# A six-layer decoder on one Trainium2 core: half of the Newton iteration's head pairs no longer cross the TensorE array

## The reference

```
def iterative_inv(mat, n_iter=6):
    I, K = eye(m), mat
    V = swapaxes(K, -1, -2) / denom
    for _ in range(n_iter):
        KV = matmul(K, V)
        V = matmul(0.25 * V, 13 * I - matmul(KV, 15 * I - matmul(KV, 7 * I - KV)))
    return V
SV = matmul(matmul(kernel1, iterative_inv(kernel2)), matmul(kernel3, V))
```

## Time and profile before

| what | value |
|---|---|
| median of three runs | 2584.53 us |
| profiled execution, its own time | 2582.42 us |
| its span | 2580.6 us |
| TensorE busy | 2279.9 us, 88% |
| VectorE busy | 1957.8 us, 76% |
| ScalarE busy | 1443.2 us, 56% |
| GpSimd busy | 360.0 us, 14% |
| mean granted TensorE clock | 0.951 of full |
| ScalarE copies of crossed groups (lines 993, 1004) | 150.9 + 129.5 us |

### The profile page before, as it was taken

One profiled execution on the slowest core, in us unless ns is written; L12 is line 12 of the kernel. 1 busy time (PEld: TensorE's weight loads), 2 busy tenths in 40 slices (PEclk: granted clock), 3 DMA queues, 4 the chain that ended last, 5 costly groups with the idle time before them and its releaser, 6 DMA issues.

```text
span 2580.6 us, 95561 instructions
## 1 busy us (share of the span) xinstructions
PE 2279.9 (88%) x40576; PEld 1845.7 (72%) x40576; DVE 1957.8 (76%) x6185; ACT 1443.2 (56%) x5093; POOL 360.0 (14%) x516
## 2 busy tenths in 40 slices
PE   6589999999999999999999999999999999999875
PEld 4467777777777777777777777777777777777763
DVE  3358887887888887788888777888877788887753
ACT  0346565655665556566555655655565565656531
POOL 0001111111111111111111111111111111111111
PEclk9589999999999999999999999999999999999995
DMA  6000000000000000000000000000000000000000
GB/s 267 5 4 7 9 9 8 9 9 5 7 9 9 9 9 9 5 7 8 8 9 8 9 5 8 8 8 9 8 9 5 8 8 9 9 8 7 4 5 3
DMA packets 29529, 35.73 MB, mean 14 GB/s; under 512 B 3240, under 2 KB 27824, under 8 KB 28464
## 3 DMA queue, kind: packets, MB, share of 16 engines
q1 hardware_dynamic: 29104, 29.62, 3.3%
HBM read 27.51 MB, written 2.10 MB: 11 GB/s over the span
## 4 chain that ended last, share of the span: by engine, by line
PE 44%; DVE 29%; ACT 18%; issue 6%; POOL 1%; DVEq 0%; ACTq 0%; POOLq 0%
PE ps L525 23%; PE ps L528 7%; ACT probs L1079 5%; PE ps L785 3%; ACT ss L993 3%; PE ps L869 3%; PE ps L802 3%; DVE probsT L1322 2%; ACT probs L1027 2%; PE ps L917 2%; ACT ey L1004 2%; DVE small L1227 2%; DVE x_rows L1186 2%; DVE small L1315 2%; DVE qk_v L1310 1%
## 5 line engine op out<-in xcount | busy, mean ns | idle before, releaser
L1027 ACT ACTIVATE probs<-ps,small 128x128 f32<-128x128 f32 x1024 | 282.5, 391 | 70.1 <-DVE small L1315 69.2
L1322 DVE COPY probsT<-ps 128x512 f32<-128x512 f32 x384 | 262.8, 684 | 75.8 <-PE ps L528 72.7
L1112 POOL TENSOR_TENSOR small<-small,weights 128x1 f32<-128x1 f32 x256 | 140.6, 549 | 1178.7 <-DVE small L1175 1178.7
L528 PE MATMUL ps<-weights,probs 128*128 128x128 f32 x1536 | 248.0, 284 | 47.1 <-POOL probs L1123 23.8
L1315 DVE TENSOR_REDUCE small<-ps 128x4 f32<-128x512 f32 x384 | 254.1, 683 | 13.0 <-PE ps L869 8.7
L528 PEld LDWEIGHTS ps<-weights,probs 128*128 128x128 f32 x1536 | 171.3, 142 | 110.4 <-POOL probs L1123 45.0
L1123 POOL TENSOR_TENSOR probs<-probs,small 128x256 f32<-128x256 f32 x128 | 108.9, 851 | 927.2 <-DVE small L1451 927.2
L1079 ACT ACTIVATE probs<-ps,small 128x128 f32<-128x128 f32 x512 | 181.3, 371 | 14.5 <-DVE small L1315 13.0
L525 PE MATMUL ps<-wz,ss 64*64 64x72 f32 x6144 | 156.0, 228 | 17.6 <-DVE wz L1269 12.2
L1268 DVE SCALAR_TENSOR_TENSOR wz<-ey,ss 128x256 f32<-128x256 f32 x320 | 147.1, 460 | 31.0 <-ACT ss L993 13.5
L989 ACT COPY ss<-ps 128x288 f32<-128x288 f32 x192 | 77.4, 403 | 158.8 <-PE ps L525 156.7
(11 more groups left out here) (200 smaller groups left out, 5288.3 us busy)
## 6 DMA issues: line engine op xcount, KB each, us to landing
weights<-in_wpack SPq DMA_DIRECT2D x1, 5703.5 KB
fc_B<-in_b SPq DMA_DIRECT2D x2, 2048.0 KB, 13.5
fc_A<-in_a SPq DMA_DIRECT2D x2, 2048.0 KB, 23.4
x_in_rows<-in_x SPq DMA_DIRECT2D x32, 64.0 KB, 1.8
x_in_T<-in_xT SPq DMA_DIRECT2D x32, 64.0 KB, 1.8
ctx_T<-in_ctxT SPq DMA_DIRECT2D x32, 64.0 KB, 1.9
ctx_rows<-in_ctx SPq DMA_DIRECT2D x32, 64.0 KB, 1.9
mask_i<-in_mask SPq DMA_DIRECT2D x32, 64.0 KB, 1.9
```

The source lines that it names most:

```text
L528: return nc.tensor.transpose(dst, src, ident)
L1027: ins = nc.scalar.activation(probs(s, g)[:, j], bank(s, SCORE_BANK[g], 128 * j, 128), ACT.Exp, bias=sm(s, "nb", 4 * g + j, 1), scale=-1.0)
L1112: nc.gpsimd.tensor_tensor(sm(s, out), sm(s, ve), w("mhalf"), ALU.pow).then_inc(sem(done, s), 1)
L1322: V.tensor_copy(probsT(s, n % 4).rearrange("p a b -> p (a b)"), bank(s, 2)).then_inc(sem("pT", s), 1)
```

## The change

The products of pairs 4 to 7 go straight as well, so only two of the four quadrants of the array are used. S and W now run group by group: the eight products of group 0, a signal, then the eight of group 1, a signal. Each group has its own wait in front of it (S of group g waits for ScalarE's copy and VectorE's Y of group g only, W for the `wz` of group g). ScalarE copies each group with one instruction of 128 partitions. `newton_ps` counts 25 a batch instead of 13; the waits of VectorE are renumbered.

```
-                for i in range(4):
-                    for g in range(2):
-                        p = 4 * g + i
-                        for m in range(2):
-                            mm = one(PS[s][halves[m ^ g], g, PW * i:PW * i + PW], ey[halves[m], p, 0:M], ey[halves[m], p])
-                mm.then_inc(sem("newton_ps", s), 1)
+                for g in range(2):
+                    if k:
+                        pe.wait_ge(sem("newton_act", s), at("newton_act", s, 4 * (k - 1) + g + 3))
+                        pe.wait_ge(sem("newton_dve", s), at("newton_dve", s, 4 * (k - 1) + g + 6))
+                    for i, p in enumerate(range(*GROUPS[g])):
+                        for m in halves:
+                            mm = one(PS[s][m, g, PW * i:PW * i + PW], ey[m, p, 0:M], ey[m, p])
+                    mm.then_inc(sem("newton_ps", s), 1)
                 yield f"n.S{k}"
...
+                for g in range(2):
+                    pe.wait_ge(sem("newton_dve", s), at("newton_dve", s, 4 * k + g + 4))
+                    a = 0 if k < NEWTON - 1 else M
+                    for i, p in enumerate(range(*GROUPS[g])):
+                        for m in halves:
+                            mm = one(PS[s][m, g, PW * i + a:PW * i + PW], ss[m, p, 0:M], wz[m, p, a:PW])
+                    mm.then_inc(sem("newton_ps", s), 1)
                 yield f"n.W{k}"
...
-                act.wait_ge(sem("newton_ps", s), at("newton_ps", s, 2 * k + 1))
-                src, ps = pairs_of(0)
-                copy(ss[:, ps], src).then_inc(sem("newton_act", s), 1)
-                yield f"n.S{k}0"
-                src, ps = pairs_of(1)
-                for m in range(2):
-                    ins = copy(ss[halves[m], ps], src[halves[1 - m]])
-                ins.then_inc(sem("newton_act", s), 1)
-                yield f"n.S{k}1"
+                for g in range(2):
+                    act.wait_ge(sem("newton_ps", s), at("newton_ps", s, 4 * k + g + 1))
+                    src, ps = pairs_of(g)
+                    copy(ss[:, ps], src).then_inc(sem("newton_act", s), 1)
+                    yield f"n.S{k}{g}"
...
-PERIOD = 74.58771
+PERIOD = 74.73423
...
-        "n.kk1 25.611  n.y0 26.400  n.S0 29.609  n.W0 32.504  n.S1 35.092  n.W1 35.643  n.S2 39.321  "
+        "n.kk1 29.676  n.y0 33.113  n.S0 33.547  n.W0 35.114  n.S1 35.969  n.W1 37.672  n.S2 41.931  "
```

More of the change, by code:

```diff
@@ L64 @@
 BATCHES = B
-PERIOD = 74.58771
+PERIOD = 74.73423
 PLACES = {
     "sp": (
-        "n.xT 2.765  n.x 72.671  ",
+        "n.xT 2.753  n.x 72.659  ",
         "r1.ctxT 83.425  r1.ctx 83.485  rf.ln 233.799  ",
@@ L72 @@
     "pe": (
[16 rows of a table removed]
[16 rows of a table added]
     ),
     "act": (
[11 rows of a table removed]
[11 rows of a table added]
     ),
     "pool": (
[L104 to L107, removed]
+        "n.lm0 32.016  n.lm1 32.153  n.out 79.211  ",
+        "r1.ctx 119.834  r1.out 139.854  rm.out 150.641  r2.xbo 165.982  r2.out 194.062  ry.stats 194.063  "
+        "ry.xbo 206.175  ry.p0 209.086  ry.p1 217.087  ry.p2 219.010  ry.p3 219.627  ry.out 241.057  "
+        "rf.out 267.480  ",
     ),
     "dve": (
[17 rows of a table removed]
[17 rows of a table added]
     ),
@@ L148 @@
     "n_exp": 6, "n_first_ps": 3, "n_k2T": 1, "n_lm": 4, "n_lm_pool": 2, "n_nb": 6, "n_p2": 2, "n_qk": 2, "n_rd": 1,
-    "n_s_ps": 6, "n_v9": 1, "n_w9": 1, "newton_act": 22, "newton_dve": 27, "newton_ps": 13, "newton_u": 12, "o_ps": 1,
+    "n_s_ps": 6, "n_v9": 1, "n_w9": 1, "newton_act": 22, "newton_dve": 27, "newton_ps": 25, "newton_u": 12, "o_ps": 1,
     "proj": 3, "sub": 1, "xT": 1, "xT_in": 16, "x_in": 16, "z": 1, "zT": 1, "zT_ps": 1,
@@ L618, in nystrom @@
             for k in range(NEWTON):
[L619 to L622, removed]
-                for i in range(4):
-                    for g in range(2):
-                        p = 4 * g + i
-                        for m in range(2):
-                            mm = one(PS[s][halves[m ^ g], g, PW * i:PW * i + PW], ey[halves[m], p, 0:M], ey[halves[m], p])
-                mm.then_inc(sem("newton_ps", s), 1)
-                yield f"n.S{k}"
-                pe.wait_ge(sem("newton_dve", s), at("newton_dve", s, 4 * k + 5))
-                a = M if last else 0
-                for i in range(4):
-                    for g in range(2):
-                        p = 4 * g + i
-                        for m in range(2):
-                            mm = one(PS[s][halves[m if last else m ^ g], g, PW * i + a:PW * i + PW], ss[halves[m], p, 0:M],
-                                     wz[halves[m], p, a:PW])
-                mm.then_inc(sem("newton_ps", s), 1)
+                for g in range(2):
[6 more added lines that the diff above has]
+                    mm.then_inc(sem("newton_ps", s), 1)
+                yield f"n.S{k}"
+                for g in range(2):
[5 more added lines that the diff above has]
+                    mm.then_inc(sem("newton_ps", s), 1)
                 yield f"n.W{k}"
@@ L986, in nystrom @@
             for k in range(NEWTON):
-                act.wait_ge(sem("newton_ps", s), at("newton_ps", s, 2 * k + 1))
-                src, ps = pairs_of(0)
-                copy(ss[:, ps], src).then_inc(sem("newton_act", s), 1)
-                yield f"n.S{k}0"
-                src, ps = pairs_of(1)
-                for m in range(2):
-                    ins = copy(ss[halves[m], ps], src[halves[1 - m]])
-                ins.then_inc(sem("newton_act", s), 1)
-                yield f"n.S{k}1"
-                if k < NEWTON - 1:
-                    act.wait_ge(sem("newton_ps", s), at("newton_ps", s, 2 * k + 2))
-                    act.wait_ge(sem("newton_u", s), at("newton_u", s, 2 * k + 2))
-                    src, ps = pairs_of(0)
-                    nc.scalar.mul(ey[:, ps], src, 0.25).then_inc(sem("newton_act", s), 1)
-                    yield f"n.W{k}0"
-                    src, ps = pairs_of(1)
-                    for m in range(2):
-                        ins = nc.scalar.mul(ey[halves[m], ps], src[halves[1 - m]], 0.25)
-                    ins.then_inc(sem("newton_act", s), 1)
-                    yield f"n.W{k}1"
+                for g in range(2):
[3 more added lines that the diff above has]
+                    yield f"n.S{k}{g}"
+                if k < NEWTON - 1:
+                    for g in range(2):
+                        act.wait_ge(sem("newton_u", s), at("newton_u", s, 2 * k + g + 1))
+                        act.wait_ge(sem("newton_ps", s), at("newton_ps", s, 4 * k + g + 3))
+                        src, ps = pairs_of(g)
+                        nc.scalar.mul(ey[:, ps], src, 0.25).then_inc(sem("newton_act", s), 1)
+                        yield f"n.W{k}{g}"
             tail_zT(s, 1)
@@ L1279, in nystrom @@
                     else:
-                        dve.wait_ge(sem("newton_ps", s), at("newton_ps", s, 2 * k + 2))
+                        dve.wait_ge(sem("newton_ps", s), at("newton_ps", s, 4 * k + g + 3))
                         ins = V.scalar_tensor_tensor(Y, src[:, :, M:PW], 0.25, uy[:, ps], ALU.mult, ALU.add)
@@ L1283, in nystrom @@
                     yield f"n.W{k}{g}"
-            dve.wait_ge(sem("newton_ps", s), at("newton_ps", s, 2 * NEWTON + 1))
+            dve.wait_ge(sem("newton_ps", s), at("newton_ps", s, 4 * NEWTON + 1))
             v = bank(s, 0, 0, 128).rearrange("p (a b) -> p a b", b=16)[:, :, 0:HD]
```

## The result

The changed kernel takes 2568.77 us (median of four runs, 2567.0 to 2571.27) against 2585.91 us for the kernel before (four runs). The ratio is 0.9936 with a 95% interval from 0.9922 to 0.9949: 0.6% faster. The forecast was 2592 us, 0.3% slower. The time lies inside the range, but the sign was wrong. The profiled execution took 2567.0 us with a span of 2565.2 us, 15.4 us less than before.

A forecast was written before the change was run, and what follows sets the result against it. It took in-order lists waiting for one another as the bound, TensorE nearest to full (88% busy). The terms 82 + 17 - 65 - 26 + 0 gave +8 us, forecast 2592 us against 2584.5, range 2553 to 2655.

The forecast's parts named there:

- the multiplication by 32: Costs and gains read from one steady batch were taken for all 32 batches, such as 5 x 32 chain blocks.
- I take 0 for the order and keep -14 to +14: New order of TensorE's list: counted as 0 us in the sum, with ends of -14 and +14 us.
- the scores ahead of the first S: Stream 1's scores, moved from behind the first S: their 0.44 us wait for o_rows could cost 14 us at most.
- The other place: Transposes that waited 0.41 us for GpSimd, moved behind the third W: up to 13 us back if they held W.
- Signalling by group: ScalarE's copy of group 0 runs beside group 1's products, at two chain points a batch: -26 us.
- Plain copies: One 128-partition ScalarE copy replaces two of 64 for the crossed group: half of 129 us on the chain, -65 us.
- The chain and cover terms: Longer S and W blocks on TensorE, 0.51 us each: +82 us for 160 on the chain, +17 for 192 partly covered.
- What would show it: Expected trace signs: S and W blocks of 1.0 to 1.2 us, TensorE busy 130 to 180 us more, ScalarE 138 less.
- The rival of the one bank: In S and W, one PSUM bank takes one row half at a time: some 540 us more, 3124 us; chance 0.02.
- The rival of TensorE as the bound: TensorE's idle time can't absorb the longer blocks, so the off-chain part costs its full 70 us: 2645 us; chance 0.27.
- The rival of the iteration's latency: The iteration's latency was the bound and off-chain additions vanish in cover: 2553 to 2567 us, named 2560; chance 0.19.

The follow-up runs named there:

- the filler products: Kernel before the change, with four more 128x128 products behind each S and W of the first batch, into an unread PSUM bank: 2595.65 us, ratio 1.0039.
- e3: Changed kernel, but S and W wait once for both groups and signal once after both; straight products, plain copies, new order kept: 2699.28 us, ratio 1.0435.
- e9: Changed kernel, but group 1 crosses again and ScalarE copies it in two pieces; split signals and new order kept: 2604.11 us, ratio 1.0074.

## Why the prediction was wrong, point by point

**The step that failed first is the multiplication by 32.** The prediction read one steady batch and said "the same pattern in each batch"; every term of its sum is a term of the steady part. The first distance, in whose iteration TensorE is busy for 3.72 of 10 us at a clock of 0.50, was not looked at. There the chain runs through every half step, so the split and the plain copies shorten each of them, and the clock, which has no term in the sum, rises for part of the iteration. Together they give 14.6 us, and 5.7 more in the second batch, where the sum had +0.25 us a batch. This turns the sign: without it the changed kernel would be 5.3 us slower in these two executions. That this is close to the +8 forecast for all batches is luck, as the next points show.

**"I take 0 for the order and keep -14 to +14".** The order is worth 62 us to the new code (2630.64 to 2568.77). One place that the prediction named, the scores ahead of the first S, carries that much and more; it was priced at a loss of up to 14 us. The error was to price the moved block by the wait seen ahead of it. What counted was the wait that it covers at its new place, and the half step that its successor covers. The other place, priced at a gain of up to 13 us, is worth nothing.

**"Signalling by group", -26 us.** The runs show 130 us. I counted only two points of the chain. That is in the new order, which was not priced with it. With longer blocks every half step is longer without the split (7.22 against 4.48 us for two of them at the start), and that the new order suits only the short one is my reading of it.

**"Plain copies", -65 us.** Measured 35 us, of which 9.6 are at the start and partly clock.

**The chain and cover terms, +82 and +17 us.** The block was sized rightly: 1.15 us measured, 1.17 forecast. In the old order the changed code needs 77.01 us a batch against 74.91, so the code's net in the steady part is +2.1 us a batch where the sum had +0.25. Two errors of 60 us, one here and one in the order, cancelled each other. That the steady part ended near the forecast (74.97, forecast 74.9, against 74.91 before and not the 74.6 that the prediction took over all batches) is therefore luck and no merit of its terms.

**What would show it.** ScalarE's busy time was to fall to 1305 us and fell to 1273.3, TensorE's was to rise by 130 to 180 us, less what the modelled tails hid, and rose by 109. The blocks came out as named.

**The rival of the one bank fell.** 72-column blocks of both row halves in one bank take 1.15 us, not 2.2. The rival of TensorE as the bound was right about the place of the chain (71%), wrong about the price. The rival of the iteration's latency had the sign right and came nearest in size (2553 to 2567 us, 2568.77 measured), but put the gain in the steady part; it was given 0.19.

## What to carry to other kernels

A kernel with a ramp has two bounds: read the first batches as a stage of their own before a term is multiplied by the count of batches, since a latency that the steady part hides is bare there. Where engines take their work in a fixed order, code and order are one design: price an edit in the order that goes with it, and a moved block by the wait that it covers where it now stands. A clock that is at its lower level is a term of its own: read it before and after, and do not count on more work to raise it, since the filler products did and the long blocks with one signal did not.

## What the runs showed of the hardware that I had not expected

A stage can get faster although its blocks of products get longer. The changed kernel's blocks of batch 0 kept TensorE busy for 2.19 us at the half clock, against 1.24 before, and each full step still took 4.48 us instead of 6.13. The full clock came where split signals and plain copies left hardly a wait between these blocks (1.00, with 8.44 us busy from 88 to 98 us), but not with the long blocks alone: it is 0.50, with 5.56 us busy, in e3, and 0.50, with 7.04, in e9. With four quadrants in flight a product of 64x64 quadrants goes at 16.4 ns an instruction from start to start at the full clock, with two at 32 ns, and both row halves writing one bank did not slow it. A steady batch of the kernel before takes 1.2 us more when it holds 3.4 us at the half clock, with TensorE full ahead of the fall. And one moved block in an in-order list can cost 3%: 2568.77 to 2650.58 us.
